# Narrow score matmuls set between wide ones in the TensorE order of a gated attention and feed-forward block

## The reference, cut to what matters

```python
def attention(q, latent_kv, Wq, Wkv_expand, Wout):          # 16 heads (NH) of 32 (HD)
    qp = q @ Wq.T
    kv = latent_kv @ Wkv_expand.T
    k, v = jnp.split(kv, 2, axis=-1)
    qh, kh, vh = (heads(a) for a in (qp, k, v))             # b, 16, 256, 32
    scores = jnp.einsum('bhqd,bhkd->bhqk', qh, kh) / jnp.sqrt(32.0)
    scores = jnp.where(causal, scores, lowest)
    out = jnp.einsum('bhqk,bhkd->bhqd', softmax(scores), vh)
    return merge(out) @ Wout.T

x = x + jnp.tanh(g_xattn[0]) * attention(layernorm(x), ctx_512, Wq, Wkv_expand, Wout)
x = x + jnp.tanh(g_ffn[0]) * ffn(layernorm(x), w_gate_up, w_down)   # silu(gate) * up, values rounded to 8-bit steps
```

## Time and profile before

| | |
|---|---|
| median of three runs | 758.56 us (756.11 to 759.13) |
| profiled execution | 758.76 us |
| its span, first to last instruction | 756.8 us |
| TensorE matmuls (PE) busy | 710.4 us, 94% |
| TensorE weight loads (PEld) busy | 511.7 us, 68% |
| VectorE (DVE) busy | 622.6 us, 82% |
| GpSimd (POOL) busy | 578.7 us, 76% |
| ScalarE (ACT) busy | 413.2 us, 55% |
| DMA queue of the heads, shares of 16 engines | 72.3% |
| mean granted TensorE clock | 0.984 |

### The profile page before, as it was taken

One profiled execution on the slowest core, in us unless ns is written; L12 is line 12 of the kernel. 1 busy time (PEld: TensorE's weight loads), 2 busy tenths in 40 slices (PEclk: granted clock), 3 DMA queues, 4 the chain that ended last, 5 costly groups with the idle time before them and its releaser, 6 DMA issues.

```text
span 756.8 us, 16991 instructions
## 1 busy us (share of the span) xinstructions
PE 710.4 (94%) x5321; PEld 511.7 (68%) x5345; DVE 622.6 (82%) x1894; ACT 413.2 (55%) x657; POOL 578.7 (76%) x766
## 2 busy tenths in 40 slices
PE   3699799999999999999999999998999999999993
PEld 3677788888878888888788886656444444444441
DVE  3796587887888978978978868699999999999982
ACT  5457457568476576576585572464444344344340
POOL 5558569788788797787787875678888888888884
PEclk9799999999999999999999999999999999999998
DMA  9897676876876977977968759973566665565565
GB/s 263 226 242 197 169 190 173 225 197 190 213 205 180 242 173 196 241 182 209 210 181 214 159 140 223 272 147 76 128 161 141 136 159 133 138 162 131 140 147 164
DMA packets 137919, 137.59 MB, mean 182 GB/s; under 512 B 90317, under 2 KB 99815, under 8 KB 137703
## 3 DMA queue, kind: packets, MB, share of 16 engines
q1 hardware_dynamic: 136768, 135.97, 72.3%
q10 hardware_dynamic: 1063, 0.54, 0.4%
HBM read 40.24 MB, written 25.31 MB: 87 GB/s over the span
## 4 chain that ended last, share of the span: by engine, by line
PE 58%; issue 12%; POOL 11%; DMA 8%; DVE 5%; SPq 4%; ACT 1%; POOLq 0%; ACTq 0%; DVEq 0%
PE psum L1554 10%; PE psum L1576 9%; PE psum L1618 9%; PE psum L1507 5%; PE psum L1935 5%; POOL hidden L776 5%; PE psum L1592 4%; PE psum L1505 4%; POOL y L790 3%; PE psum L1541 3%; DMA x1b<-x_scratch 3%; PE psum L1564 3%; POOL hq L783 2%; PE psum L1945 2%; DMA heads<-nmT 2%
## 5 line engine op out<-in xcount | busy, mean ns | idle before, releaser
L1181 DVE CUSTOM_DVE_ANT_0 junk<-psum,mask 128x128 f32<-128x128 f32 (+1 forms) x512 | 153.6, 354 | 66.9 <-PE psum L1507 65.0
L1935 PE MATMUL psum<-w1q,xqb 128*128 128x512 bf16 (+1 forms) x755 | 156.7, 361 | 2.1 <-DVE u L1222 1.4
L776 POOL TENSOR_TENSOR hidden<-hidden 128x512 f32<-128x512 f32 (+1 forms) x96 | 112.5, 1187 | 29.0 <-ACT hidden L1109 28.7
L891 ACT ACTIVATE prob<-psum 128x768 f32<-128x768 f32 x128 | 103.6, 810 | 52.5 <-PE psum L1594 50.7
L1935 PEld LDWEIGHTS psum<-w1q,xqb 128*128 128x128 bf16 x768 | 74.4, 98 | 80.2 <-DVE u L1222 1.6
L1114 ACT ACTIVATE hidden<-hidden,round_bias,hinv 128x1408 f32<-128x1408 f32 x32 | 49.9, 1561 | 113.8 <-DVE hinv L1460 113.8
L591 POOL TENSOR_SCALAR_AFFINE_SELECT prob<-prob 128x512 f32<-128x512 f32 x128 | 81.7, 640 | 32.8 <-ACT prob L891 31.1
L599 POOL TENSOR_TENSOR prob<-prob 128x256 f32<-128x256 f32 x128 | 98.0, 771 | 6.2
L1945 PE MATMUL psum<-w2q,hqT 128*128 128x512 bf16 x341 | 80.7, 385 | 6.7 <-DMA hqT<-hq 6.2
L1554 PE MATMUL psum<-xT_hi,wq_hi 128*128 128x256 f32 x256 | 75.0, 293 | 4.7 <-POOL xT_lo L606 2.8
L1507 PE MATMUL psum<-heads 96*128 96x256 f32 x256 | 76.7, 335 | 0.0
(11 more groups left out here) (116 smaller groups left out, 1792.6 us busy)
## 6 DMA issues: line engine op xcount, KB each, us to landing
heads<-k_hi SPq DMA_DIRECT2D x128, 128.0 KB, 4.5
heads<-q_hi SPq DMA_DIRECT2D x128, 128.0 KB, 4.3
xln<-x_dram SPq DMA_DIRECT2D x16, 512.0 KB, 5.9
heads<-k_lo SPq DMA_DIRECT2D x64, 128.0 KB, 4.0
heads<-q_lo SPq DMA_DIRECT2D x64, 128.0 KB, 3.9
x<-x_dram SPq DMA_DIRECT2D x16, 512.0 KB, 4.2
x_scratch<-x SPq DMA_DIRECT2D x16, 512.0 KB, 4.2
x1b<-x_scratch SPq DMA_DIRECT2D x32, 256.0 KB, 3.4
```

What stands on the lines that cost most here:

```text
L776: pool.tensor_tensor(up[t % 3][:, o], gate[t % 3][:, o], up[t % 3][:, o], ALU.mult).then_inc(f["prod_done"], 1)
L891: act.activation(prob[:, g % 2, pair % 2, 0:CAUSAL // P].rearrange("p k h q -> p h k q"), psum[:, 2:4, 0:CAUSAL].rearrange("p h (k q) -> p ...
L1181: dve.tensor_tensor_reduce(junk[:, n % 2, 0:w], psum[:, h % 2, cols], m, 1.0, LOWEST, ALU.add, ALU.max, mx[:, X % 2, t, h:h + 1]).then_inc ...
L1935: last = pe.matmul(psum[:, bank, 0:w], xqb[:, t % 4, k, :], w1q[:, k, half * I + o:half * I + o + w], start=(k == 0), stop=(k == KH - 1))
```

## The change

Two places of every full slot are written anew for TensorE; the other engines' lists stay as they are, and so do the opening, the ending and the tiles. No matmul is added or taken away.

First, the two calls of `values` with `score_pair(b, 1)` between them become one `values_and_pair`: the four matmuls of the pair stand one by one behind the first four of the six matmuls of the values. All the waits (both banks of the values, the exponential of pair 0) stand ahead of the first of them. Second, `scores` of heads 13 and 14, the first half of the first output tile, and `scores` of head 15 become one `output_and_scores`: the six matmuls of the three heads stand one by one behind the six of the output. The waits for the output's bank and for `o_lo` stand ahead of all, those for `max_done` ahead of each head.

```diff
+                def output_and_scores(X, Y, first):
+                    bank = work_bank(pe, X, "O", 0)
+                    pe.wait_ge(s["o_lo"], 2 * X + 1)
...
+                    for g in range(2):
+                        for n, (oo, w) in enumerate(((o_hi, wo_hi), (o_lo, wo_hi), (o_hi, wo_lo))):
+                            pe.matmul(psum[:, bank, :], oo[:, g, o], w[:, g, :], start=(g == n == 0), stop=False)
+                            i = 3 * g + n
+                            h = first + i // 2
+                            if i % 2 == 0:
+                                wait_for(pe, s["max_done"], 2 * (NHEAD * Y + h - 1))
+                                early_scores(Y, h)
+                            else:
+                                late_scores(Y, h)
+                def values_and_pair(X, Y, pair):
+                    banks = [work_bank(pe, X, "V", t) for t in range(ST)]
+                    pe.wait_ge(s["exp_done"], PAIRS * Y + pair)
+                    for t in range(ST):
+                        o = slice(t * P, (t + 1) * P)
+                        for n, (cc, w) in enumerate(((c_hi, wkv_hi), (c_lo, wkv_hi), (c_hi, wkv_lo))):
+                            last = pe.matmul(psum[:, banks[t], :], cc[:, o], w[:, H:2 * H], start=(n == 0), stop=(n == 2))
+                            if n == 2:
+                                last.then_inc(s["v_done"], 1)
+                            if t == 0:
+                                if n == 1:
+                                    late_pair(Y, pair, 0)
+                                else:
+                                    early_pair(Y, pair, n // 2)
+                            elif n == 0:
+                                late_pair(Y, pair, 1).then_inc(s["st_done"], 1)
...
-                    values(b + 1, 0)
-                    score_pair(b, 1)
-                    values(b + 1, 1)
+                    values_and_pair(b + 1, b, 1)
...
-                    scores(b + 1, 13)
-                    scores(b + 1, 14)
-                    output(b - 1, 0, 0)
-                    scores(b + 1, 15)
+                    output_and_scores(b - 1, b + 1, 13)
```

More of the change, by code:

```diff
@@ L1503, in scores, with early_scores, late_scores @@
                         wait_for(pe, s["max_done"], 2 * (NHEAD * X + h - 1))
[L1504 to L1508, removed]
+                        early_scores(X, h)
+                        late_scores(X, h)
+                def early_scores(X, h):
+                    K = 3 * HD
+                    pe.matmul(psum[:, h % 2, 0:P], qs[0:K, X % 2, h, 0:P], ks[0:K, X % 2, h, 0:P],
+                              start=True, stop=True)
+                def late_scores(X, h):
+                    K = 3 * HD
+                    pe.matmul(psum[:, h % 2, P:CAUSAL], qs[0:K, X % 2, h, P:S], ks[0:K, X % 2, h, 0:S],
+                              start=True, stop=True).then_inc(s["s_done"], 1)
                 def maxima_rows(X):
@@ L1579, in output @@
                             last.then_inc(s["o_done"], 1)
+                def output_and_scores(X, Y, first):
+                    bank = work_bank(pe, X, "O", 0)
+                    pe.wait_ge(s["o_lo"], 2 * X + 1)
+                    if X == 0:
+                        pe.wait_ge(s["split"], 3)
+                    o = slice(0, P)
+                    for g in range(2):
[8 more added lines that the diff above has]
+                                late_scores(Y, h)
@@ new lines, in early_pair, with late_pair @@
+                def early_pair(X, pair, d):
+                    K = 3 * HD + 2
+                    h, bank = 2 * pair + d, 2 + d
+                    early = psum[:, bank, 0:CAUSAL].rearrange("p (k q) -> p k q", q=P)[:, 0:3:2, :]
+                    pe.matmul(early, ks[0:K, X % 2, h, 0:P], qs[0:K, X % 2, h, 0:S].rearrange("p (k q) -> p k q", q=P),
+                              start=True, stop=True)
+                def late_pair(X, pair, d):
+                    K = 3 * HD + 2
+                    h, bank = 2 * pair + d, 2 + d
+                    return pe.matmul(psum[:, bank, P:S], ks[0:K, X % 2, h, P:S], qs[0:K, X % 2, h, P:S],
+                                     start=True, stop=True)
@@ L1587, in score_pair @@
                     wait_for(pe, s["exp_done"], PAIRS * X + pair)
-                    K = 3 * HD + 2
                     for d in range(2):
[L1590 to L1595, removed]
+                        early_pair(X, pair, d)
+                        last = late_pair(X, pair, d)
                     last.then_inc(s["st_done"], 1)
```

## The result

The changed kernel took 774.78 us (median of 4 runs, 771.51 to 776.98) against 757.97 us before (median of 4): ratio 1.0207, 95% interval 1.0178 to 1.0236. The medians lie 16.8 us apart; by the ratio it is slower by 2.1%. The forecast was 771.8 us in a range of 764.5 to 776.5.

The account below looks back on a forecast made before the run. TensorE was taken to bound the kernel, busy 29.23 of 29.30 us per slot. Values' stall 10.7, output wait 1.7, head 15 and GpSimd 0.6, neighbours 0: 13.0 us on 758.76 gives 771.8 us, range 764.5 to 776.5.

Parts of the forecast that it names:

- The values' term: Values and pair 1: waits moved ahead of their cover stall TensorE 0.65 to 1.16 us per slot, 10.7 us over 13.
- The low edge of this term: Values' stall if the restart costs nothing beyond the 0.05 us to the load: given as 9.5 us.
- rival B: Score loads' waits for VectorE's maxima, 8.3 us in 39 pieces, absorb part of the delay: 763.5 us; chance 0.08.
- The output's term: Output block: wait for `t_copied` moved ahead of heads 13 and 14 costs 0.14 us in 12 slots, 1.7 us.
- part of 0.6: Head 15's wait for head 13's maxima and GpSimd's chain to `weigh(b, 0)` together: 0.6 us of a possible 0 to 1.8.
- rival C: Pair 1's late exponential, uncovered, delays `weigh(b, 0)` 0.3 us per slot: +3.5 us, about 775 us; chance 0.08.
- The gain of the new neighbours: Alternating wide and narrow matmuls hides no load: 0 taken, -3.4 us kept as the end of the range.
- A: Alternating blocks: the stall comes but narrow loads are hidden as well, 768.4 us; chance 0.12.
- D: Faster than before: loads hidden and no stall at the values, 755.4 us; chance 0.03.
- E: Interleaving changes nothing, both waits met by slack hidden in modelled matmul starts: 758.8 us; chance 0.03.
- The wider reading of the Trainium skill's rule on the reorder window: Alternating blocks: loads pulled more than one ahead would hide narrow loads, saving 3.4 us over 13 slots.

Follow-up runs that it names:

- the waits alone: Kernel before with both bank waits and the wait for pair 0's exponential put ahead of the first value, no matmul moved: 773.37 us, ratio 1.0180.
- the pair in the second tile: Kernel before with pair 1 after a whole first values tile, head 1's matmuls among the second tile's, each wait covered: 760.25 us, ratio 1.0023.
- the values part alone: Changed kernel with the output and heads 13 to 15 put back as before, values and pair 1 still alternating: 773.03 us, ratio 1.0192.
- the output part alone: Changed kernel with values and pair 1 put back as before, output and heads 13 to 15 still alternating: 760.68 us, ratio 1.0025.
- the output block covered: Kernel before with heads 14 and 15 put between output matmuls, head 13 ahead and both small waits covered: 759.62 us, ratio 1.0005.
- head 15 earlier: Kernel before with head 15 behind the fourth output matmul instead of the sixth: 760.11 us, ratio 1.0008.
- the three with fills: Unread matmuls in slot 1's pauses: changed kernel (both pauses) 774.47 us; first pause only, kernel before 757.71 us, that with head 15 earlier 756.99 us.

## Why the prediction was right, and where its sizes were off

**Direction and cause: right.** The named step was the wait for `q_lo` (and the exponential in one or two slots) put ahead of the work that covered it. The trace has the 13 stops, and the kernel with the waits alone shows that they suffice.

**The values' term, 10.7 us: too small by about 1.5.** In the slots the part from the broadcast to the end of the values grew by 0.94 us on average over slots 2 to 13 (40.4 against 29.1 us, +11.3), where I had read 9.8. For slots 3, 5 and 6 I had read a delay of about 0.7 us, because there TensorE itself had been held by the DMA ahead of pair 0. In the changed kernel it was not held there, and the part grew by about 1.05 us: that is 1.1 of the 1.5. (The low edge of this term was 9.3 us, not 9.5: 13 x 0.11 us off 10.7.)

**The wait for the DMA ahead of pair 0, which I left as it was.** It fell by 2.4 us between the two profiles. Part of that could be a small piece of rival B, though by another wait than I named: a slot is now paced by VectorE's chain from head 15 to `q_lo`, so TensorE's delay for a DMA ahead of pair 0 comes off its stop for `q_lo`: the values end 3.10 to 3.13 us behind the broadcast in the three slots with such a wait, and 3.41 in most others. But the fall can't be put down to the change. From the matmul ahead of pair 0 to the broadcast, slots 3 to 13 together took 9.6 us (5.9 of it without any wait) in the profile of the kernel before, 7.2 in the changed one, and 6.8 to 8.0 in the six other profiles without a stop in every slot. So most of the 2.4 us is that the profiled execution of before had longer waits than these.

**The output's term, 1.7 + part of 0.6.** 0.20 us per slot, 2.6 us over 13: 0.13 for `t_copied`, as read, and the rest, about 0.07, for the maxima of head 13, where I had 0.06 or nothing. GpSimd's part of the 0.6 did not come in the changed kernel (rival C), though `weigh` came only 0.02 to 0.04 us short of it; the kernel with the pair in the second tile showed that wait.

**The gain of the new neighbours, 0.** Right: wide plus narrow is 0.35 us in the orders tried, so rivals A and D had no basis, and E fell with the stops themselves. The wider reading of the Trainium skill's rule on the reorder window ("TensorE: Matmul & The Clock Gate", section "Architectural detail: the array is 16× 32×32, not 1× 128×128") is not borne out here: also in the changed order each load begins when the matmul before it does, none goes two ahead.

**What was missing: the clock in slot 1.** I wrote "The clock, granted at 1.00 over a slot, I leave where it is". That held in slots 2 to 13 and failed in slot 1, where the stop for `q_lo` is 2.15 us, because ScalarE makes the high queries late (VectorE is idle 5.27 us for them), and follows a stop of 2.19 us. Slot 1 took 4.3 us more, of which the forecast had about 1.0; some 3 us are matmuls at the 1.2 GHz level (6.8 us at half the pace). That the change causes this is not shown. With the waits put ahead in slot 1 and no fill, the clock fell there in all three profiles (the changed kernel, the values part alone, the waits alone), and with each wait ahead of its own user as well. But with the old order it fell for 6.8 us too in the kernel with the output part alone and in the one with the output block covered, whose slot 1 then took 33.73 and 32.80 us, and for 3.4 us with slot 1 alone in the old order and with the pair in the second tile. It stayed up in the kernel before, with head 15 earlier, and in the three with fills. So the 3 us may in part, or in the main, be the luck of two executions.

Sum against the profiled run: 8.9 + 0.9 (values in slots 2 to 13 less the DMA's waits, and in slot 1) + 2.6 (output) + 3 (clock) - 0.8 (start and ending) = 14.6 us, where 13.0 were forecast. That the sum is so near is luck in part: the values' stops were 1.5 us too small and the clock was missing, and the DMA's waits and the ending made up for most of it. The ending of the kernel before had 3.4 us at clock 0.50 (from 470.1 us), that of the changed kernel none. The medians moved 16.8 us; for the 2.2 us between I have no cause, and one execution of each kernel can't tell how that shift divides between waits and clock to better than 2 or 3 us.

## What to carry to other kernels

A block that is fused from two pieces inherits the latest of their waits at its first instruction; before fusing, read from the timeline when each wait is released and what work stands between it and its user, because that work is the cover. For the matmuls of this kernel the cost of a matmul with its load did not depend on its neighbours (one load ahead, started with the matmul before), so the order was free to be chosen by the waits alone. A pause of TensorE cost its length in slots 2 to 13, where it was about 1 us; around pauses of 2 to 4 us the clock could fall, and 6.8 us at half the pace cost some 3 us more. Whether it does has to be looked up in several profiles, not in one.

## What the runs showed of the hardware that was not expected

- With matmuls of 512 and of 128 or 256 columns in turn, fp32r, loads of 128 columns: 0.35 us per couple (0.23 + 0.12), the same as in blocks of one kind.
- The clock fell to 0.50 for 6.8 us in the second of two idle times of 2.19 and 2.15 us with 1.20 us of work between. The lengths of the pauses alone do not decide it: in slot 1 of the kernel before, idle times of 3.00 and 0.81 us left it at 1.00, and with the output block covered, idle times of 2.94 and 0.79 us came with 0.50 for 6.8 us; one of 3.67 us, with slot 1's values in the old order, came with 0.50 for 3.4 us. Of the kernel with the output block covered this is a window, the stretch between its two pauses:

```profile
82.00:84.00 2.00, 1.95 (x8) 1.13 (x6) 0.00 (x0) 0.61 (x2) 0.00 (x0) 0.57 0.28 68
```

- The mean clock of a run goes along with its time (0.971 to 0.989 over all runs here). With the output part alone, 11 runs reach from 756.11 us at 0.986 to 766.24 us at 0.974.
